# First slots of an attention kernel: the second group's inputs loaded ahead of the output weights, whose raw copy lies in V's buffer and in half of the scores', and the sums of V's weights on VectorE

## The reference

```python
q, k, v = heads(x @ Wq + bq), heads(x @ Wk + bk), heads(x @ Wv + bv)
scores = einsum('bhqd,bhkd->bhqk', q, k) / sqrt(32)
scores = where(mask == 0, -inf, scores)
out = einsum('bhqk,bhkd->bhqd', softmax(scores), v)
y = x + out.transpose(0, 2, 1, 3).reshape(b, s, 512) @ Wo + bo
return (y - mean(y)) / sqrt(var(y) + 1e-5)
```

## Time and profile before

| | |
|---|---|
| median of 3 runs | 811.19 us (809.91 to 812.51) |
| profiled execution | 811.64 us, of which the span from the first to the last instruction is 809.5 us |
| mean granted TensorE clock | 0.999 |
| busy: PE | 800.8 us (99%) |
| busy: DVE, POOL, ACT | 642.8, 551.4, 267.1 us (79%, 68%, 33%) |
| chain that ended last | PE 93%, DVE 2%, DMA 2%, POOL 1% |

### The profile page before, as it was taken

How to read it: one execution, slowest core, us unless ns; L and a number is a source line. 1 busy time by engine, 2 the same in 40 slices (tenths; PEclk the granted TensorE clock), 3 DMA queues, 4 the chain that set the end, 5 groups by cost and what they waited for, 6 DMA issues and landing times.

```text
span 809.5 us, 26951 instructions
## 1 busy us (share of the span) xinstructions
PE 800.8 (99%) x11771; PEld 679.1 (84%) x11771; DVE 642.8 (79%) x1002; ACT 267.1 (33%) x349; POOL 551.4 (68%) x443
## 2 busy tenths in 40 slices
PE   9999999999999999999999999999999999999997
PEld 7778888888888888888888888888888888888876
DVE  5968778787778887887877788877878777876895
ACT  6533333323333223332233332233322333323223
POOL 1797778666687666786667767667866668755672
PEclk9999999999999999999999999999999999999999
DMA  9334545254352534534345344444435435234342
GB/s 330 125 80 121 162 119 160 84 154 142 106 183 79 161 118 119 177 98 142 115 114 177 115 129 124 146 146 117 156 88 163 122 116 176 75 105 117 96 107 103
DMA packets 64965, 106.62 MB, mean 132 GB/s; under 512 B 11728, under 2 KB 28624, under 8 KB 62672
## 3 DMA queue, kind: packets, MB, share of 16 engines
q1 hardware_dynamic: 52368, 87.85, 34.7%
q10 hardware_dynamic: 12480, 17.06, 8.1%
HBM read 54.53 MB, written 16.78 MB: 88 GB/s over the span
## 4 chain that ended last, share of the span: by engine, by line
PE 93%; DVE 2%; DMA 2%; POOL 1%; SPq 1%; issue 0%; ACT 0%; POOLq 0%; DVEq 0%
PE ring L367 15%; PE ring L369 14%; PE ring L368 14%; PE ring L519 7%; PE ring L520 7%; PE ring L523 7%; PE psum_s L470 6%; PE psum_s L440 6%; PE ring L461 6%; PE psum_s L472 6%; PE psum_s L474 6%; DMA x_raw<-in_xt 2%; DVE x_lo L885 0%; DVE wo_lo L1014 0%; POOL soft L232 0%; POOL soft L1178 0%
## 5 line engine op out<-in xcount | busy, mean ns | idle before, releaser
L1178 POOL TENSOR_TENSOR soft<-soft,top 128x1024 f32<-128x1024 f32 x62 | 123.4, 1991 | 22.1 <-DVE top L950 22.1
L232 POOL TENSOR_TENSOR soft<-soft,inverse 128x1024 f32<-128x1024 f32 x62 | 118.8, 1918 | 25.9 <-DVE inverse L957 25.8
L954 DVE TENSOR_REDUCE total<-soft 128x16 f32<-128x1024 f32 x62 | 75.2, 1213 | 48.8 <-ACT soft L713 48.8
L367 PE MATMUL ring<-x_hi,wk_hi 128*128 128x512 f32 x256 | 103.2, 403 | 1.6 <-DVE v L891 1.3
L713 ACT ACTIVATE soft<-soft 128x1024 f32<-128x1024 f32 x62 | 65.8, 1062 | 111.6 <-POOL soft L1178 111.6
L369 PE MATMUL ring<-x_hi,wk_lo 128*128 128x512 f32 x256 | 99.9, 390 | 0.0
L368 PE MATMUL ring<-x_lo,wk_hi 128*128 128x512 f32 x256 | 99.7, 389 | 0.0
L519 PE MATMUL ring<-wo_hi,ot_hi 128*128 128x512 f32 x252 | 99.1, 393 | 0.0
L520 PE MATMUL ring<-wo_lo,ot_hi 128*128 128x512 f32 x252 | 98.9, 392 | 0.0
L748 ACT CAST s_hi<-v 128x1024 fp32r<-128x1024 f32 x27 | 28.3, 1047 | 207.4 <-DVE v L903 207.4
L367 PE MATMUL ring<-x_hi,wq_hi 128*128 128x512 f32 x248 | 96.6, 389 | 0.0
(11 more groups left out here) (125 smaller groups left out, 1878.2 us busy)
## 6 DMA issues: line engine op xcount, KB each, us to landing
pt<-soft SPq DMA_DIRECT2D x248, 64.0 KB, 2.5
x_raw<-in_xt SPq DMA_DIRECT2D x15, 1024.0 KB, 6.8
row<-in_x SPq DMA_DIRECT2D x60, 256.0 KB, 2.7
out_rows<-row SPq DMA_DIRECT2D x60, 256.0 KB, 2.4
pt<-soft ACTq DMA_DIRECT2D x232, 64.0 KB, 2.3
v<-in_xt SPq DMA_DIRECT2D x27, 512.0 KB, 4.6
adj<-in_adj SPq DMA_DIRECT2D x16, 128.0 KB, 2.7
kt<-in_wk SPq DMA_DIRECT2D x4, 256.0 KB, 5.7
```

The source lines that it names most:

```text
L232: ops.tensor_tensor(soft_of(c), soft_of(c), on_keys(inverse[:, c % 2, :]), ALU.mult).then_inc(normed, 1)
L367: nc.tensor.matmul(out, left_hi, right_hi, start=kc == 0, stop=False)
L954: nc.vector.tensor_reduce(total[:, c % 2, :], by_row_head(soft_of(c)), AX_XY, ALU.add).then_inc(summed, 1)
L1178: nc.gpsimd.tensor_tensor(soft_of(c), soft_of(c), on_keys(top[:, c % 2, :]), ALU.subtract).then_inc(centred, 1)
```

## The change

- SP issues the second group's inputs (`load_x(1)`) and pair 1's (`load_pair(1)`) ahead of Wo, and Wo in two halves of 512 KB: chunks 2 and 3 into `soft[:, 1]`, then chunks 0 and 1 into `v[:, 0:2]`. Half of `soft`, tile 0's, is no longer used for it.
- `add_weights`, the four raw sums of Wv's blocks, goes from GpSimd to VectorE, between the second group's `x_lo` and `add_inputs(1)`.
- ScalarE casts these sums right behind `read_k(2)`, then does `read_k(3)`, then casts chunks 2 and 3 of Wo; chunks 0 and 1 are cast in slot 0, between `read_q(4)` and `exp(0)`.
- VectorE makes the low parts of chunks 2 and 3 behind `add_inputs(1)`, and those of chunks 0 and 1 in slot 0, between `sum_up(0)` and `sum_up(1)`.
- One warm-up matmul less.

```diff
-WARM_START = 9
+WARM_START = 8
...
-        w_raw = [qt[:, 1], kt[:, 1], row[:, :, :],
-                 soft[:, :, :, :, :].rearrange("p a b h k -> p (a b h k)").rearrange("p (c n) -> p c n", n=D)]
+        wo_raw = [v[:, 0:2, :], soft[:, 1].rearrange("p b h k -> p (b h k)").rearrange("p (c n) -> p c n", n=D)]
+        w_raw = [qt[:, 1], kt[:, 1], row[:, :, :]]
+        WO_ORDER = (2, 3, 0, 1)
+
+        def w_raw_chunk(n, kc):
+            return wo_raw[kc // 2][:, kc % 2, :] if n == 3 else w_raw[n][:, kc, :]
...
             load_adj(0)
-            sp.dma_start(w_raw[3], w_dram[3]).then_inc(w_in[3], DMA)
             load_x(1)
             load_pair(1)
+            for half in (1, 0):
+                sp.dma_start(wo_raw[half], w_dram[3][:, 2 * half:2 * half + 2, :]).then_inc(w_in[3], DMA)
...
             read_k(2)
-            split_w(3, 0)
-            split_w(3, 1)
-            read_k(3)
-            split_w(3, 2)
-            split_w(3, 3)
             for n in range(4):
                 split_weight_sums(n)
+            read_k(3)
+            split_w(3, WO_ORDER[0])
+            split_w(3, WO_ORDER[1])
...
                     read_q(a + GT)
+                    if p == 0:
+                        split_w(3, WO_ORDER[2])
+                        split_w(3, WO_ORDER[3])
                     exp(a)
...
             for c in range(GT, 2 * GT):
                 split_x(c)
-            split_w(3, 0)
-            split_w(3, 1)
+            add_weights()
             add_inputs(SEVEN.start)
-            split_w(3, 2)
-            split_w(3, 3)
-            dve.wait_ge(w_lo_done, 5 * KC)
+            split_w(3, WO_ORDER[0])
+            split_w(3, WO_ORDER[1])
+            dve.wait_ge(w_lo_done, 4 * KC + 2)
...
                 sum_up(a)
+                if p == 0:
+                    split_w(3, WO_ORDER[2])
+                    split_w(3, WO_ORDER[3])
                 sum_up(b)
...
                 else:
+                    dve.wait_ge(w_lo_done, 5 * KC)
                     read_v(a)
                     read_v(b)
...
             make_bias(0)
-            add_weights()
             split_weight_sums()
```

More of the change, by code:

```diff
@@ L763, in split_w @@
                     act.wait_ge(wk_in[kc], DMA)
+                elif n == 3:
+                    act.wait_ge(w_in[3], 2 * DMA)
                 elif kc == 0:
                     act.wait_ge(w_in[n], DMA)
-                nc.scalar.copy(w_hi[n][:, kc, :], w_raw[n][:, kc, :]).then_inc(w_hi_done, 1)
+                nc.scalar.copy(w_hi[n][:, kc, :], w_raw_chunk(n, kc)).then_inc(w_hi_done, 1)
             for kc in range(KC):
@@ L903, in add_inputs, with add_weights @@
                 nc.vector.tensor_tensor(at(x, 0, 1), at(x, 0, 1), at(x, 0, 0), ALU.subtract).then_inc(s_raw_done, 1)
+            def add_weights():
+                dve.wait_ge(w_in[2], DMA)
+                for n, left, right, op, done in (
+                        (0, w_raw_block(0, 1), w_raw_block(0, 0), ALU.subtract, 0),
+                        (2, w_raw_block(1, 1), w_raw_block(0, 1), ALU.subtract, 0),
+                        (1, w_raw_block(1, 1), t_raw(0), ALU.subtract, 1),
+                        (3, w_raw_block(1, 0), t_raw(1), ALU.subtract, 3)):
+                    wait_for(dve, t_raw_done, done)
+                    nc.vector.tensor_tensor(t_raw(n), left, right, op).then_inc(t_raw_done, 1)
             def quarter(m, i, j):
@@ L1012, in split_w @@
             def split_w(n, kc):
-                dve.wait_ge(w_hi_done, (n + 1) * KC + kc + 1)
-                nc.vector.tensor_tensor(w_lo[n][:, kc, :], w_raw[n][:, kc, :],
+                dve.wait_ge(w_hi_done, (n + 1) * KC + (WO_ORDER.index(kc) if n == 3 else kc) + 1)
+                nc.vector.tensor_tensor(w_lo[n][:, kc, :], w_raw_chunk(n, kc),
                                         w_hi[n][:, kc, :].bitcast(F32), ALU.subtract).then_inc(w_lo_done, 1)
@@ L1145, in make_bias @@
                     0.0, MASKED, ALU.is_equal, ALU.mult).then_inc(bias_done, 1)
[L1147 to L1153, removed]
-                        (3, w_raw_block(1, 0), t_raw(1), ALU.subtract, 3)):
-                    wait_for(pool, t_raw_done, done)
-                    nc.gpsimd.tensor_tensor(t_raw(n), left, right, op).then_inc(t_raw_done, 1)
             def split_weight_sums():
```

## The result

| | before | with the change |
|---|---|---|
| median | 810.68 us (6 runs, 809.91 to 812.51) | 815.88 us (6 runs, 814.27 to 816.76) |
| ratio, 95% interval | | 1.0059 (1.0044 to 1.0075) |
| profiled execution | 811.64 us, span 809.5 us | 816.3 us, span 814.2 us |
| mean granted TensorE clock | 0.999 | 0.996 |

The change makes the kernel 0.6% slower. The forecast was 812.3 with a range up to 814.0.

The account below looks back on a forecast made before the run. TensorE's own pace bounds the 809.5 us span, apart from short waits; only the start of project_k(6) moves the end. 811.64 + 1.15 = 812.8, or 812.3 against 811.19; range 810.3 to 814.0.

Parts of the forecast that it names:

- +1.15 us: Slot 0: the two wo_lo delay sum_up(1), and 5.42 us later project_k(6) starts at 50.57 instead of 49.41.
- the head: Stretch up to mask(0): GpSimd starts 1.86 earlier, an extra turn costs 1.55, so mask(0) comes 0.3 earlier, at 34.8.
- four operations caught: Before mask(0): third and fourth add_inputs and both wo_lo each stand behind one t_lo, against three before; a turn is 1.55 us.
- The rule of the Trainium skill: Slot 0: the shared port pair locks for the whole instruction, so the second wo_lo waits for all of normalise(0); 2.15 us taken.
- Rival A: Before mask(0): the third add_inputs escapes the t_lo, mask(0) 1.2 earlier, sum -0.05, time 811.1; chance 0.22.
- Rival B: First slot: the locks don't bite, project_k(6) follows V at once, -1.9, time 809.3; chance 0.12, wholly or in part.
- Worth 0: Start of TensorE: one warm-up matmul less takes 0.44 us off the queue, but x_hi at 8.40 stays; no gain.
- Worth 0 by itself: DMA queue: swapping Wo and the second group's inputs brings the inputs at about 20.5 instead of 23.06; no gain alone.
- Everything after is common: 0: After slot 0 and the next pair's dependent work: nothing differs between the kernels, 0 us.
- rival C: Behind the gap before project_k(6), about 3.0 us: TensorE's clock falls to 1.2 GHz, time 814.2; chance 0.08.
- +1.9: Matmuls behind the gap at half clock: nine in 4.00 us against 2.07, on top of +1.15.
- From there to the end no wait appears: TensorE from project_k(6) at 49.41 on: no wait, so whatever moves that start moves the end by as much.

Follow-up runs that it names:

- turns: Changed kernel with the two low parts in slot 0 left out (a zero stands for them) and two 128x512 transposes on VectorE in their place; 812.18 us, ratio 1.0005.
- before_two: Kernel before plus two 128x512 SBUF subtractions on VectorE between sum_up(0) and sum_up(1), nothing of the change; 814.31 us, ratio 1.0027.
- spread: Changed kernel with slot 0's two low parts moved, one ahead of sum_up(0), one between read_v(0) and read_v(1); 812.47 us, ratio 1.0003.
- spread_bo: The spread kernel with GpSimd's add_bo(0) ahead of centre(0) in the first slot; 811.68 us, ratio 0.9995.
- tlo_dve: The spread_bo kernel with the four t_lo on VectorE behind add_inputs(1), GpSimd starting its first slot after the two wo_lo; 809.50 us, ratio 0.9975.
- dma_only: Kernel before with only the second group's and pair 1's inputs issued ahead of the raw Wo; 812.47 us, ratio 1.0007.
- warm9: Changed kernel with nine warm-up matmuls instead of eight; 815.28 us, ratio 1.0038.
- pool_sums: Changed kernel with add_weights, the sums of V's weights, back on GpSimd; 813.30 us, ratio 1.0018.
- all_ahead: Changed kernel with casts and low parts of Wo's chunks 0 and 1 ahead of slot 0, behind chunks 2 and 3; 814.60 us, ratio 1.0034.

## Why the prediction was wrong

**The chain: right.** "+1.15 us" for the start of `project_k(6)` was 0.99. Its steps held: first masking 34.45 (said 34.8), last sum 27.29 (27.45), first t_lo 28.03 (28.2), four operations caught, `sum_up(1)` 45.00 (45.15), then 5.40 (5.42), a wait of 2.96 (2.5 to 3.2). Two small errors work against each other: the head gave back 0.68 and not 0.3, and the two operations cost the chain 1.67 and not 1.5. The second wo_lo took 2.41, above the 2.15 taken and just above the upper bound of 2.3, while `normalise(0)` itself grew to 2.38; turns and before_two together show that it is the alternation with GpSimd that makes it. The rule of the Trainium skill (SBUF — State Buffer, the section on the two separate sides) stood behind that value, and the 2.41 beside GpSimd's two-input operation agrees with it. It doesn't hold beside every GpSimd operation: next to the one-input comparison of the mask a wo_lo took 0.67 in spread, spread_bo and tlo_dve, and there the measurement decides.

That 0.99 came so close to 1.15 is partly luck, since 49.41 is one execution's: the forecast took the fourth `add_inputs` of the kernel before as caught, and two other traces with the old code around it (before_two, dma_only) have it uncaught and the first masking at 33.74 and 34.01. Against those the change moves `project_k(6)` by 2.1 to 2.4 us (from 48.31, and from 48.0 by the estimate), not 1. How often each comes isn't known.

**Rival A fell**: the third `add_inputs` was caught (1.48). **Rival B fell**: the wo_lo took 3.46, not 1.24. **"Worth 0"** for the warm-up matmul is shown for the chain by warm9's unchanged start of `project_k(6)`; for the clock's return it isn't shown. "Worth 0 by itself" for the order of the transfers holds for the measured time (dma_only: 1.0007, 0.9991 to 1.0023).

**The step that failed is the term for the matmuls behind the gap, which the sum of 812.3 put at nothing.** "Everything after is common: 0" let them run at full pace; in the profiled execution fourteen of them ran at half the clock and took 2.8 us more. That term was priced only in rival C, with too small a weight and then too small a size. The text had the mechanism, and had the gap right ("from 1.3 to about 3.0 us"). It gave 0.08 to "If the clock falls to its lower level (1.2 GHz of 2.4) in that gap", on the ground that "No row shows a gap of 3 us". The absence of a row speaks neither way, and 0.08 treated it as evidence against. Of the six executions of the change four have a mean clock of 0.994 to 0.997, as only 5 of the 105 later executions of the kernel before have; two have 0.998, which doesn't tell. All six took 814.27 us or more. The mean is blurred by the end of the run: in the kernel before the granted clock is 0.72 from 806.0 to 809.5 us, where TensorE has no work. The price, "+1.9", took the nine warm-up matmuls as the count of slow ones; the pace was right (0.43 against 0.44) but the count is what the clock makes of it: fourteen in this execution, 2.8 us, and seven in warm9, 1.4 us. With the two measured terms the sum is 811.19 + 0.99 + 2.8 = 815.0, just above the 814.2 of rival C and outside the range.

The rest to the measured 815.88 isn't explained: 1.1 us of the profiled execution arise behind 681 us, where the kernels vary among themselves. The prediction's "From there to the end no wait appears" passes over a wait of 0.6 us at 775.90 in the kernel before ("L461 <- issue"). The kernel before measured 810.68 in the comparison with the change and 811.68 to 812.03 in the later ones, so about 1 us of the first ratio may be chance; warm9, the change but for one matmul, has 3.3 us.

## What to carry to other kernels

When a change lengthens a wait of a TensorE that otherwise hardly waits, count the wait and then the matmuls at half rate behind it. Here waits of 1.8 to 3 us cost 1.4 to 2.8 us more, and filler matmuls in the gap, or moving the work, took it back. A two-input SBUF operation on VectorE is priced by what GpSimd does at that moment: 0.6 us alone, 1.7 beside GpSimd's 128x512 subtractions (3.46 for two), 2.4 beside its 128x1024 one. Idle time of VectorE is room for it only where GpSimd is idle too or the operation is of another kind, and several of them back to back on one engine took less than in turns with the other (tlo_dve). Before two traces are compared by a microsecond, look whether a stretch of unedited code differs by as much; here one did, by 1.4 us.

## What the runs showed of the hardware that I had not expected

- The granted clock fell behind gaps of 1.81, 1.85, 2.05, 2.94 and 2.96 us, and not behind those of 1.29 to 1.70 us. Behind 1.81 and 2.05 it fell 1.0 us after TensorE had gone back to work, and behind 1.85 after the first matmul, 0.3 us. Each is one profiled execution; the mean clocks of before_two's ten executions (0.994 to 1.0) suggest both outcomes for one kernel.
- The slow stretch lasted 3.1 us (warm9), 3.4 to 3.7 (pool_sums, before_two, all_ahead) and 6.1 us (the change), with TensorE busy throughout.
- The alternation also holds up GpSimd: `normalise(0)` behind a turn of VectorE took 2.38 us instead of 1.92, in the change and in before_two alike.
- A two-input operation of VectorE was not held up by GpSimd's one-input comparison (128x256): 0.67 us in spread, spread_bo and tlo_dve, against 0.62 with GpSimd idle.
- In the kernel before the granted clock is 1.00 from 1.30 to 5.30 us, while the nine warm-up matmuls there start 0.44 us apart. So at the start of the run the granted clock of the profile doesn't tell the pace; the starts of the matmuls do.
